# Moving PE's transpose of a finished group's sums from the fourth to the sixth tile of the next group

## What is computed

```python
msgs = edge_vals[:, None] * x[edge_src]                 # layer 0
agg = jax.ops.segment_sum(msgs, edge_dst, num_segments=N)
...
agg = jax.ops.segment_sum(norm[:, None] * xW[src], dst, num_segments=n_nodes)   # layer 1, in each of two convolutions
```

## Time and profile before

| what | us |
|---|---|
| median of 3 runs | 3854.28 (3852.82 to 3855.93) |
| span of the profiled execution, core 0 | 4334.5 |
| first aggregation, from its first gather to its last | 106.3 to 1254.4 |
| second and third | 1815.0 to 4114.0 |
| PE busy in the span | 2842.8 |
| POOL busy in the span | 2524.5 |
| mean granted TensorE clock | 0.827 of full |

### The profile page before, as it was taken

The page is one execution under the profiler, slowest core; times in us unless marked ns, Lnnn a source line. Parts: engine busy times, 40 slices in busy tenths (PEclk is TensorE's granted clock), DMA queues, the critical chain, the costliest instruction groups (busy, mean ns, idle before and its releaser), DMA issues. The chain is left out here.

```text
span 4334.5 us, 42515 instructions
## 1 busy us (share of the span) xinstructions
PE 2842.8 (66%) x12338; PEld 2151.9 (50%) x12338; DVE 1865.2 (43%) x5797; ACT 795.6 (18%) x1977; POOL 2524.5 (58%) x2689
## 2 busy tenths in 40 slices
PE   3577767777777566646656656555476767767678
PEld 2455545555544544435545545444354555555557
DVE  6343446666646823513322222222244444444443
ACT  1111101111113223301111111100022222232230
POOL 4666666666630533666666666665666666666601
PEclk9788879888888788978878778776788888888878
DMA  5333334444432466634333333332333333333305
GB/s 156 101 111 105 108 94 121 124 128 118 120 90 87 151 200 196 208 108 119 116 101 108 108 108 107 102 98 82 89 107 108 106 107 110 103 110 109 104 21 180
DMA packets 279543, 501.74 MB, mean 116 GB/s; under 512 B 59771, under 2 KB 179969, under 8 KB 279162
## 3 DMA queue, kind: packets, MB, share of 16 engines
q0 software_dynamic: 126240, 345.85, 27.7%
q1 hardware_dynamic: 135916, 139.10, 10.4%
q10 hardware_dynamic: 17136, 13.84, 1.0%
HBM read 419.12 MB, written 79.18 MB: 115 GB/s over the span
## 5 line engine op out<-in xcount | busy, mean ns | idle before, releaser
L1401 POOL DMA_INDIRECT g<-d_t,src_i x1568 | 1506.9, 961 | 806.4 <-issue 483.4
L1473 PE MATMUL bank<-g,m 128*128 128x256 f32 (+1 forms) x4704 | 1440.7, 438 | 94.3 <-issue 45.4
L1473 PEld LDWEIGHTS bank<-g,m 128*128 128x128 f32 x4704 | 943.0, 221 | 307.3 <-issue 141.2
L1401 POOL DMA_INDIRECT g<-d_xn,src_i x784 | 766.0, 977 | 389.2 <-issue 223.7
L1426 DVE TENSOR_SCALAR m<-iota,rel_f,ew_f 128x128 f32<-128x128 f32 x2352 | 702.0, 362 | 383.3 <-DMA d_xs<-zero 170.3
L1461 PE MATMUL bank<-ident,s 128*128 128x128 f32 x588 | 144.0, 334 | 438.3 <-ACT s L1407 390.2
L1437 DVE TENSOR_TENSOR accT<-bank,accT 128x256 f32 x294 | 121.9, 415 | 628.8 <-remote 269.8
L1407 ACT ACTIVATE s<-bank 128x256 f32<-128x256 f32 (+1 forms) x294 | 111.7, 380 | 1338.4 <-DMA nb<-d_deg 435.6
L1461 PEld LDWEIGHTS bank<-ident,s 128*128 128x128 f32 x588 | 86.3, 166 | 495.2 <-ACT s L1407 425.9
L1425 DVE TENSOR_SCALAR eq<-iota,rel_f 128x128 bf16<-128x128 f32 x784 | 227.5, 290 | 182.9 <-remote 140.3
L1435 DVE TENSOR_TENSOR dinv<-bank,dinv 2x128 f32 x98 | 27.1, 276 | 319.4 <-remote 310.0
(11 more groups left out here) (386 smaller groups left out, 4235.9 us busy)
## 6 DMA issues: line engine op xcount, KB each, us to landing
g<-d_t,src_i POOLq DMA_INDIRECT x1568
side_xn<-d_xn SPq DMA_DIRECT2D x96, 256.0 KB
g<-d_xn,src_i POOLq DMA_INDIRECT x784
d_swT<-wkv SPq DMA_DIRECT2D x48, 256.0 KB
swT<-d_swT SPq DMA_DIRECT2D x24, 512.0 KB, 3.7
xt<-d_xs POOLq DMA_DIRECT2D x80, 128.0 KB, 2.9
d_ys<-y ACTq DMA_DIRECT2D x80, 128.0 KB, 2.5
x<-in_x SPq DMA_DIRECT2D x24, 256.0 KB, 2.8
```

The costliest lines, as they stand in the source:

```text
L1401: pool.indirect_dma_start(g[n % RING][:, u, 0:D], None, table, bass.IndirectOffsetOnAxis(ap=k.src_i[:, t:t + 1], axis=0)).then_inc(gathere ...
L1473: ins = pe.matmul(b[:, 0:GW], m[o][:, u, :], g[r][:, u, :], start=(u == 0), stop=(u == GT - 1 and not count))
```

## The change

`turn_window(n - 1)`, the transpose of the last group's sums, stands behind the sixth tile of group n instead of the fourth:

```diff
--- before.py
+++ after.py
@@ -1480,7 +1480,7 @@
                     n = 2 * i + slot // GT
                     if n < NG:
                         tile(n, slot % GT)
-                    if slot % GT == 3 and 0 < n <= NG:
+                    if slot % GT == 5 and 0 < n <= NG:
                         turn_window(n - 1)
                     at_step(side.pe, slot, i)
```

## The result

| kernel | median, us | lowest to highest | runs |
|---|---|---|---|
| before | 3853.26 | 3841.49 to 3855.93 | 5 |
| after | 3868.84 | 3860.03 to 3875.15 | 5 |

The ratio is 1.0044, with a 95% interval of 1.0032 to 1.0055: the change makes the kernel **slower by 0.4%, 15.6 us**. The forecast was 3855, no difference, and the range ended at 3863.

A forecast was written before the change was run, and what follows sets the result against it. The prediction took the kernel as POOL-bound, 1.25 us a gather without waits for buffers, with PE behind. It added 0.6 us for the drain to 3854.3, its other terms being 0, giving 3855 us, range 3847 to 3863.

The forecast's parts named there:

- the sum of 3862.0: Whole kernel: 2352 gathers at 1.2525 us, 2945.9, plus 916.1 for the rest, without any wait of POOL.
- PE's wait for ACT: PE waiting for ACT's copy: 390.2 + 62.6 us in 78 cases of the profile, taken as absent in the runs.
- "faster" rival: PE's 78 waits for ACT are real and shrink by 0.86 to 1.77 us each: 3787 to 3716; chance 0.06.
- The shorter cover in Slices: PE's turn3 (L1290) waits 1.31 us more in 49 rounds; cost 0, upper bound 64 us.
- the drains: End of each stage, after the last tile: bounds 0 to 1.8 us, taken as 0.6.
- the wait that now stands in front: Transpose and DVE's finish come up to four gathers, 5.0 us, later, covered by PE's 10 us in hand; cost 0.
- gathers stretched: Rival: shifted DVE steps lengthen one more gather a round in Slices, 25 us, 3880; chance 0.03.
- the span of 4335: Profile after the change: the profiled execution's span was expected to stay near 4335 us.
- 430 us of POOL's waits: Profile after the change: POOL's waits for free buffers were expected again, some 430 us net.

The follow-up runs named there:

- E1: The kernel before, unchanged, run again for a second profile: 3851.82 us, ratio 0.9999 to before.
- E4: The kernel before with the transposes late in the Slices stage only: 3852.95 us, ratio 1.0003.
- E3: The kernel before with the transposes late in the Between stage only: 3851.95 us, ratio 1.0002.
- E2: The kernel before with the transposes late in the first stage (LinearAttention) only: 3864.66 us, ratio 1.0044.
- E9: E2 plus one small DVE memset in front of the one-hot steps in 17 rounds: 3861.06 us, ratio 1.0032 to before.
- E15: The kernel before with DVE held ahead of finish's add in 17 first-stage rounds until PE used up the next group: 3875.04 us, ratio 1.0064.
- E13: E2 plus a DVE wait for its own add behind finish in the first stage: 3848.15 us, ratio 1.0000 to before.
- E10: E2 plus four small DVE memsets in front of the one-hot steps in 17 rounds: 3851.66 us, ratio 1.0004 to before.
- E14: The changed kernel plus a DVE wait for its own add behind finish in the first stage: 3853.20 us, ratio 1.0010 to before.
- E8: The changed kernel with DVE's one-hots ahead of its place-a side steps in the first stage: 3854.20 us, ratio 1.0016 to before.
- E16: E15 plus a DVE wait for its own add behind finish in the first stage: 3849.08 us, ratio 0.9997 to before.

## Why the prediction was wrong

**What held.** The kernel is POOL-bound without waits for buffers, as the sum of 3862.0 had it against a measured 3853; E1 spans 3848.2 and POOL's idle time before gathers there is turnaround and the gaps between the stages. That the sum comes so close is in part luck: by the rows of E1, counted in the same way, the gathers' stretches take 2973.5 us where the sum had 2945.9, and the rest 874.7 where it had 916.1, so two misses cancel for the most part. What the earlier trace rows were taken to mean for the runs held too: the 390.2 + 62.6 us of PE's wait for ACT are 0.3 + 0.5 in E1, so there was nothing to win, and the "faster" rival fell (its 1.77 us at half the clock should be 2 x 0.86 = 1.72, on which nothing hung). Why that one execution waited is not shown. The shorter cover in Slices came, and was as harmless as forecast, in the view of waits of after (engine, line, released by, us, times, longest):

```profile
POOL g L1401 <- issue: 745.3, 2311, 22.6
PE bank L1473 <- DMA g<-d_t,src_i: 548.2, 325, 12.4
...
PE bank L1290 <- DVE wg L1284: 36.2, 49, 1.4
```

and in E1:

```profile
PE bank L1290 <- DVE wg L1284: 3.1, 3, 1.4
```

After has 49 waits of PE at L1290, one a round, of 36.2 us together against an upper bound of 64: 0.74 us each where 1.31 was the estimate, the longest 1.4. E4 shows no price for them that can be told (1.0003). PE still waits for gathers. Between and the drains cost nothing that can be told either (E3, E4).

**What failed.** Two steps. The first is the sentence on *the wait that now stands in front*: it followed the later add into DVE's order, asked only whether PE's cover would hold, and put "cost on the path: 0". The cover did hold. What the later add does to DVE itself was not asked: the pause between `finish` and the next steps closes, and DVE runs from the add through L635 and L619 into the burst, 5.4 us without a pause in the rows of after. Gathers are held there: eight of them, 13.9 us, in E2. The second is the rival *gathers stretched*. It had the right resource, but was priced in Slices, at one row of 1.46 us, and given 0.03 because "these steps meet one gather either way". The length of what a gather meets is not fixed: the same steps cost it little when they come apart (the longest gather of E1 is 0.6 above 0.95), and up to 2.8 when they come without a pause. The earlier trace rows held a warning that I did not use: its first stage has a longest gather of 2.417 us, where the other two have 1.474, and that gather is one of the six above. Put right after the fact, the sum is the forecast plus some eight held gathers of 0.8 to 2.8 us (E2's least and greatest over 1.6, 1.76 and 3.73, less 0.95), 6 to 22 us; the runs say 15.6. The rows taken from before do not tell how many there would be, though its trace held six.

The expectations of the profile after were wrong in one more point: neither the span of 4335 nor 430 us of POOL's waits came again. They belong to that one execution, whose mean granted clock was 0.827; that of E1 was 0.902.

The Trainium skill, "SBUF — State Buffer", section "SBUF: two separate sides", says that DVE and GpSimd share one pair of ports as an exclusive lock: of a GpSimd operation and a DVE operation that runs in a two-port mode (or has two SBUF inputs, where the GpSimd operation reads SBUF), the one that starts first keeps it for the whole instruction. The traces agree in direction: inside none of the 32 held gathers of after, E2, E9 and E15 is a one-hot step longer than 0.33 us, and where a step is drawn out, as to 0.51 in E13, the gather beside it takes 0.95. They go beyond it in length: each held gather of E2 spans 9 to 14 DVE steps. Whether the one-hot steps are operations of that kind, and whether this lock is the thing behind the rows, is not shown here.

**Still open.** Why a pause of 0.1 us behind the add decides over a burst that starts 1.2 us later; only that it does is shown. Why not every gather in an unbroken run is held (the trace of after has eight bursts behind L619 without a pause from L1435 on, and three gathers over 1.6 us in them), so where a gather starts in the run may count as well. Why E10 has no held gather: its eight runs follow the add at 0.33 us as in E2 and show no pause, and whether the 0.03 us by which the memsets delay the burst break the run or spare its gathers by the shift is not known. And whether the other two stages cost a little: E14 and E8, where the first stage is cured, are at 1.0010 with an interval from 1.0000 and at 1.0016 with one from 1.0005, while E3 and E4 alone show nothing.

## What to carry to other kernels

When POOL's gathers set the pace, a change on another engine is to be followed into the pauses of DVE, not only into the buffers: ask which DVE steps it pushes together. If a run of DVE steps becomes unbroken, look at the longest gather, not at the median, and try a wait for DVE's own last result between them; here it cost nothing that could be told (E13, E16). And take a second profile before building a sum on a first one that is 12% longer than the runs.

## What was unexpected

A gather that takes 0.95 us can take 3.73 (E2) while DVE works through 128x128 steps of 0.3 us each. The same steps, at the same offset, let it through once a pause of 0.1 us stands 1.2 us earlier (E13). The steps of E13's burst last 0.28 and 0.34 us, those of E2's 0.27 and 0.33: the kernel with the slower steps is the faster one, though which of the two is cause and which effect is not shown.
